# Softmax attention on one core: score products for the maxima on 64 rows with the two heads of a pair side by side, projections moved, the reciprocal packed, the float32 products in one block

## The chip, the cores and the metric

The kernel runs on one core of a Trainium2 chip. The metric is device time in microseconds (us) of one execution; the time of a kernel is the median of its runs. Only one of the kernel's eleven stages, the softmax attention, is changed.

## The reference

A two-layer network on x of 8 batches x 512 tokens x 128 features: a feed-forward layer with 4-bit weights, attention, feed-forward, a mixture of experts, linear attention, a mixture of experts. The changed part is the first attention:

```python
q = split_heads(x @ Wq.T)            # 16 heads of 64
k = split_heads(x @ Wk.T)
v = split_heads(x @ Wv.T)
sim = jnp.einsum('bhid,bhjd->bhij', q, k) * DIM_HEAD ** -0.5
m = jnp.max(sim, axis=-1, keepdims=True)
e = jnp.exp(sim - m)
attn = e / (jnp.sum(e, axis=-1, keepdims=True) + 1e-10)
out = jnp.einsum('bhij,bhjd->bhid', attn, v)
return out.transpose(0, 2, 1, 3).reshape(B, N, INNER) @ Wo.T + bo
```

## The kernel before

`attn_stage` works on 64 pairs of heads (8 batches, 8 pairs each). A pair has 512 queries and 512 keys for each of its two heads. Each engine runs a list of instructions in order, written out by hand as a loop over `PERIODS`; semaphores tie the lists together. In period g the stage works on five pairs at once: it projects pair g+2 (`project`, `high`, `low`, `values_in`, `to_rows`), finds the row maxima of pair g+1 (`scores`, `neg_max`, `max_turned`, `max_row`), computes the exponentials of pair g (`scores_turned`, `exp`), and sums, multiplies with the values and projects out for pairs g-1 and g-2 (`values`, `total_out`, `inv_total`, `normalise`, `output`).

What each of these does:

- `project(g, which)`: q, k or v of the pair as float16 products in high and low parts (three products of 512 columns for q and k, twelve of 128 for v) into the one PSUM bank `proj`. ScalarE's `high` writes the float16 high part, VectorE's `low` the rest, SyncE's `to_rows` copies both by ten DMAs (four of q, four of the high part of k, two of its low part) into `both`, `kh` and `kl`, in which the 128 rows hold high and low parts of a head of 64.
- `scores(g, i)`: one product of 128 queries with 512 keys, eight for a pair, into two banks in turn; VectorE's `neg_max` reduces each. `max_turned` transposes the maxima of a head, VectorE's `max_row` rounds them to `mrow`, and a DMA puts them into row 64 of `both`, so that `scores_turned` subtracts the maximum within its product.
- `scores_turned(g, i)`: keys by queries, two products into one of two banks; ScalarE's `exp` reads it into `pT`. GpSimd adds `pT` up over the keys; `values` sums over the partitions (`sums`), and multiplies `pT` with the values into `pv`, both in float32 on column halves.
- `total_out` copies the sums (128x512, each number repeated on 64 partitions), `inv_total` takes the reciprocal of all of it, `normalise` multiplies, `output` projects and accumulates over the eight pairs of a batch, `add_x` adds to x.

SyncE's list in period g is: `max_row(g, 1)`, the four DMAs of q of pair g+2, `max_row(g+1, 0)`, the six DMAs of k of pair g+2. TensorE's `values` and `output` stand in the middle of a period, after the fourth of eight `scores_turned`.

## Time and profile before

| | us |
|---|---|
| median of 3 runs (2273.93 to 2275.41) | 2275.11 |
| the profiled execution | 2278.47 |
| its span, first to last instruction | 2276.7 |
| TensorE busy in the span | 1866.1 (82%) |
| VectorE busy | 1669.5 (73%) |
| GpSimd busy | 1080.2 (47%) |
| ScalarE busy | 1066.1 (47%) |

The attention stage lies between 252 and 1154 us of the span. PE is TensorE's matmul, PEld its weight loads, DVE VectorE, ACT ScalarE, POOL GpSimd, SPq the instructions with which SyncE issues DMAs. L639 is line 639 of the kernel. A matmul's duration in the profile is longer than its share of the engine, since the next starts before it ends: the distance from one start to the next is what counts. "[0.44 <-ACT ...]" behind a line is the idle time of the engine before it and what ended it.

### The profile page before, as it was taken

The page shows a single profiled execution, that of the slowest core. Times are in us where ns is not written, and L with a number is a line of the kernel's source. Part 1 is how long each engine was busy: PE and PEld are TensorE (multiplying, and loading weights), DVE is VectorE, ACT ScalarE, POOL GpSimd, SP SyncE. Part 2 cuts the span into 40 slices and gives each one's busy share as a digit, 9 for nine tenths or more (in the row PEclk, how much of TensorE's full clock was granted, in tenths as well). Part 3 has the DMA queues.
Part 4 walks back from the last instruction along what each step waited for, and adds up shares of the span by engine and source line. Part 5 has one row for each costly group of instructions (what it writes and reads, how often), then busy time and mean ns, then how long its engine had stood idle before and what let it go on. Part 6 is the DMA issues. An engine that isn't in the chain of part 4 may idle for free. (4 is left out here: it accounts for less than half of the span.)

```text
span 2276.7 us, 36764 instructions
## 1 busy us (share of the span) xinstructions
PE 1866.1 (82%) x12205; PEld 1097.1 (48%) x12205; DVE 1669.5 (73%) x3322; ACT 1066.1 (47%) x2294; POOL 1080.2 (47%) x1304
## 2 busy tenths in 40 slices
PE   0555489999999999999935548999948888789999
PEld 0334234444444444444414435666637677656665
DVE  5887677888788877888778875666667777746665
ACT  0112255555555555555511135555537667445555
POOL 0111255555555555555611134555545556345555
PEclk9888599999999999999968977999979999879999
DMA  6000122222222222222100000000000000000000
GB/s 181 0 0 1 28 56 63 61 59 56 60 60 61 57 57 62 60 61 57 43 0 1 0 1 1 1 0 0 0 0 1 1 1 1 1 1 9 9 9 9
DMA packets 77058, 64.53 MB, mean 28 GB/s; under 512 B 12224, under 2 KB 75904, under 8 KB 76928
## 3 DMA queue, kind: packets, MB, share of 16 engines
q1 hardware_dynamic: 71392, 57.41, 9.9%
q10 hardware_dynamic: 5536, 5.52, 0.8%
q8 instruction: 67, 1.10, 0.2%
q14 instruction: 63, 0.52, 0.1%
HBM read 10.32 MB, written 2.10 MB: 5 GB/s over the span
## 5 line engine op out<-in xcount | busy, mean ns | idle before, releaser
L795 ACT ACTIVATE at_pT<-at_turned 128x512 f32<-128x512 f32 x512 | 305.6, 597 | 292.2 <-PE at_turned L862 273.3
L1022 POOL TENSOR_TENSOR m_g<-m_gT,m_g 128x512 f16<-128x512 f32 x260 | 301.4, 1159 | 232.1 <-ACT m_g L1005 232.1
L1036 PE MATMUL m_h<-m_xT,m_w 128*128 (+1 forms) x1572 | 386.8, 383 | 19.9 <-PEq L463 19.9
L694 DVE TENSOR_REDUCE at_nmax<-at_score 128x1 f32<-128x512 f32 x512 | 337.2, 680 | 71.8 <-PE at_score L839 68.7
L673 POOL TENSOR_TENSOR m_w_attn<-at_pT 128x512 f32<-128x512 f32 x128 | 162.4, 1269 | 377.1 <-ACT at_pT L795 377.1
L972 DVE TENSOR_TENSOR m_gT<-m_silu,m_h 128x512 f32<-128x512 f32 x262 | 180.3, 688 | 200.5 <-ACT m_silu L1001 200.4
L1001 ACT ACTIVATE m_silu<-m_h 128x512 f32<-128x512 f32 x262 | 156.6, 598 | 227.1 <-PE m_h L1036 227.1
L716 DVE RECIPROCAL m_w_attn<-m_w_attn 128x512 f32<-128x512 f32 x64 | 214.6, 3353 | 38.6 <-ACT m_w_attn L801 38.6
L900 PE MATMUL at_pv<-at_pT,at_v 128*64 128x512 f32 x1024 | 231.4, 594 | 0.0
L1055 PEld LDWEIGHTS m_y<-m_w,m_g 128*128 128x128 f16 x3072 | 192.9, 98 | 60.5
L1036 PEld LDWEIGHTS m_h<-m_xT,m_w 128*128 128x128 f16 x1572 | 144.3, 99 | 149.6 <-issue 28.3
L839 PE MATMUL at_score<-at_kh,at_both 128*128 128x512 f16 x512 | 197.1, 385 | 23.5 <-DVE at_nmax L694 16.8
L1055 PE MATMUL m_y<-m_w,m_g 128*128 128x128 f16 x3072 | 213.3, 219 | 0.0
L861 PE MATMUL at_turned<-at_both,at_kh 128*128 128x512 f16 x512 | 195.3, 382 | 0.4 <-ACT at_pT L795 0.3
L862 PE MATMUL at_turned<-at_both,at_kl 128*128 128x512 f16 x512 | 195.3, 381 | 0.0
L681 POOL TENSOR_TENSOR m_w_attn<-m_w_attn,at_pT 128x512 f32<-128x512 f32 x128 | 162.6, 1270 | 11.2 <-ACT at_pT L795 1.3
L677 POOL TENSOR_TENSOR m_w_attn<-m_w_attn,at_pT 128x512 f32<-128x512 f32 x128 | 162.6, 1270 | 10.6 <-ACT at_pT L795 0.8
L1005 ACT CAST m_g<-m_gT 128x512 f16<-128x512 f32 x260 | 158.6, 610 | 0.0
L349 POOL TENSOR_TENSOR f_hq<-f_hg,f_hsc 128x704 f32<-128x704 f32 x32 | 44.4, 1386 | 213.8 <-DVEq L325 213.8
L392 PE MATMUL f_gate<-m_wguT,f_xqT 128*128 128x352 f32 x128 | 61.6, 569 | 102.3 <-DVEq L321 101.0
L900 PEld LDWEIGHTS at_pv<-at_pT,at_v 128*64 128x64 f32 x1024 | 73.7, 138 | 147.6 <-issue 147.6
L987 DVE SCALAR_TENSOR_TENSOR m_x<-m_y,m_we,m_x 128x128 f32 x512 | 143.4, 343 | 0.0
(231 smaller groups left out, 3262.6 us busy)
## 6 DMA issues: line engine op xcount, KB each, us to landing
at_both<-at_part_q SPq DMA_DIRECT2D x128, 128.0 KB, 2.4
at_kh<-at_part_k SPq DMA_DIRECT2D x256, 64.0 KB, 2.0
at_both<-at_part_q SPq DMA_DIRECT2D x128, 64.0 KB, 2.0
at_kl<-at_part_k SPq DMA_DIRECT2D x128, 64.0 KB, 2.0
m_x<-in_x SPq DMA_DIRECT2D x8, 256.0 KB, 4.7
at_both<-at_mrow SPq DMA_DIRECT2D x128, 1.0 KB
out_x<-m_x SPq DMA_DIRECT2D x8, 256.0 KB, 2.3
m_wqkv<-in_w_qkv ACTq DMA_DIRECT2D x1, 1152.0 KB, 6.6
```

Source lines behind the costliest of these rows:

```text
L677: nc.gpsimd.tensor_tensor(acc, acc, pT[g % 2][:, head, 2, :], ALU.add).then_inc(chain, 1)
L694: nc.vector.tensor_reduce(nmax[head][:, qt:qt + 1], score[use % 2][:], AX.X, ALU.max, negate=True)\
L716: nc.vector.reciprocal(rinv, total).then_inc(rinv_done, 1)
L795: nc.scalar.activation(pT[g % 2][:, head, kt, :], turned[i % 2][:], ACT.Exp).then_inc(exp_done, 1)
L839: nc.tensor.matmul(score[use % 2][:], both[k][:, 0, head, qt * P:(qt + 1) * P], kh[k][:, head, :], start=True, stop=True).then_inc(s_done, 1)
L861: nc.tensor.matmul(turned[i % 2][:], kh[k][:, head, tile], both[k][:, 0, head, :], start=True, stop=False)
L862: nc.tensor.matmul(turned[i % 2][:], kl[k][:, head, tile], both[k][:, 1, head, :], start=False, stop=True)\
L900: last = nc.tensor.matmul(pv[halves[head], :], vv[g % 4][:, kt, halves[head]], pT[g % 2][:, head, kt, :], start=(kt == 0), stop=(kt == TPB ...
L972: nc.vector.tensor_tensor(gT[u % 4][:], silu[u % 2][:], h2[u % 2][:], ALU.mult).then_inc(g_done, 1)
L1022: nc.gpsimd.tensor_tensor(g16[u % 4][:, 1, :], gT[u % 4][:], g16[u % 4][:, 0, :], ALU.subtract).then_inc(low_done, 1)
L1036: last = nc.tensor.matmul(bank[:], mem["w12_16"][:, w_part, e, first:first + P], mem["xT"][:, x_part, ds(b * SEQ, SEQ)], start=(i == 0), s ...
L1055: last = nc.tensor.matmul(y[e % 2][:, tile], g16[u % 4][:, g_part, tile], mem["w3_16"][:, w_part, e, j, :], start=(j == 0 and t == 0 and i ...
```

## The change

- `scores` takes q and k from the high parts themselves (`part`, now doubled in a ring of two), 64 rows for each head, the two heads in the two row halves of TensorE and in the two banks. It waits no longer for any DMA. Before, it took q's high and low parts by the high part of k.
- Both heads' maxima go through one `max_turned` (into the bank `sums`), one `max_row` on VectorE and two DMAs, at the end of the period; `scores_turned(g, 0)` waits for both.
- q, v and k are projected after the first, fourth and sixth `scores_turned`. The sums, the output projection, the transposed maxima and the values follow each other at the end of TensorE's period.
- The reciprocal is taken of 32x32 numbers: two DMAs pack the sums, one writes the inverses to DRAM, two spread them over 64 partitions each, in the next period. `normalise` comes one period later.
- The exponents are kept 64 times smaller, and `exp` scales them back.

The core of the diff:

```diff
-        M_UNIT = 64.0
+        SHRINK = 64.0
+        SCALES = (DH ** -0.5 / W_ATTN / 4.0, 1.0 / W_ATTN / 16.0)
...
-        part = [s.sb(f"part_{n}", [P, 2, SEQ], F16) for n in "qk"]
...
-        nmax = [s.sb(f"nmax{i}", [P, P]) for i in range(2)]
-        mrow = [s.sb(f"mrow{i}", [TPB, P], F16) for i in range(2)]
-        oT = [s.sb(f"oT{i}", [P, SEQ]) for i in range(2)]
-        ones = s.sb("ones", [P, DH])
+        nmax = mem["we"][:].rearrange("p t e -> p (t e)")[:, P:2 * P]
+        mrow = s.sb("mrow", [UPP, P], F16)
+        oT = s.sb("oT", [P, SEQ])
+        ones = mem["we"][:].rearrange("p t e -> p (t e)")[:, 0:DH]
+        PACK = 32
+        packed, inv = (s.sb(n, [2 * SEQ // PACK, PACK]) for n in ("packed", "inv"))
+        inv_row = [nc.dram_tensor(f"{tag}_inv_row{i}", [2, SEQ], F32, kind="Internal").ap() for i in range(2)]
...
-        s_in = [s.sem(f"s_in{i}") for i in range(RING)]
+             "added", "sums_done", "total_done", "rinv_done", "pv_done", "o_done", "out_done", "biased", "x_added", "m_done",
+             "m_out", "packed_in", "inv_row_in", "rinv_in"))
         t_in = [s.sem(f"t_in{i}") for i in range(RING)]
-        m_in = [s.sem(f"m_in{i}") for i in range(2)]
-        S_DMAS, T_DMAS = 8, 2
+        m_in = s.sem("m_in")
+        T_DMAS = 10
...
-                    src = part[which]
...
-                def max_row(g, head):
-
-                    sp.wait_ge(s_read, turn_use(g, head) + 1)
-                    sp.dma_start(both[g % RING][DH:DH + 1, 1, head, :].rearrange("o (t q) -> o t q", q=P), mrow[head][:])\
-                      .then_inc(m_in[head], 16)
+                def max_row(g):
+
+                    sp.wait_ge(m_out, g + 1)
+                    for head in range(2):
+                        sp.dma_start(both[g % RING][DH:DH + 1, 1, head, :].rearrange("o (t q) -> o t q", q=P),
+                                     mrow[head * TPB:(head + 1) * TPB, :]).then_inc(m_in, 16)
+
+                packs = [slice(h * SEQ // PACK, (h + 1) * SEQ // PACK) for h in range(2)]
+
+                def pack_total(g):
+
+                    sp.wait_ge(total_done, g + 1)
+                    for h in range(2):
+                        sp.dma_start(packed[packs[h], :], total[h * DH:h * DH + 1, :].rearrange("o (a b) -> o a b", b=PACK))\
+                          .then_inc(packed_in, 16)
+
+                def unpack_inverse(g):
+
+                    sp.wait_ge(rinv_done, g + 1)
+                    if g >= 2:
+                        sp.wait_ge(rinv_in, 32 * (g - 1))
+                    sp.dma_start(inv_row[g % 2].rearrange("h (a b) -> (h a) b", b=PACK), inv[:]).then_inc(inv_row_in, 16)
+
+                def spread_inverse(g):
+
+                    sp.wait_ge(inv_row_in, 16 * (g + 1))
+                    if g:
+                        sp.wait_ge(o_done, g)
+                    for h in range(2):
+                        sp.dma_start(rinv[halves[h], :], inv_row[g % 2][h:h + 1, :].to_broadcast([DH, SEQ])).then_inc(rinv_in, 16)
 
                 sp.wait_ge(set_up, RING + 3)
                 for g in PERIODS:
-                    if live(g):
-                        max_row(g, 1)
+                    if live(g - 2):
+                        spread_inverse(g - 2)
                     if live(g + 2):
                         if g + 2 >= RING:
                             sp.wait_ge(t_done, 8 * (g + 3 - RING))
@@ -653,13 +670,16 @@
                         to_rows(g + 2, 0, 0)
                         sp.wait_ge(lo_done, 2 * (g + 2) + 1)
                         to_rows(g + 2, 0, 1)
-                    if live(g + 1):
-                        max_row(g + 1, 0)
-                    if live(g + 2):
                         sp.wait_ge(hi_done, 2 * (g + 2) + 2)
                         to_rows(g + 2, 1, 0)
                         sp.wait_ge(lo_done, 2 * (g + 2) + 2)
                         to_rows(g + 2, 1, 1)
+                    if live(g - 1):
+                        pack_total(g - 1)
+                    if live(g + 1):
+                        max_row(g + 1)
+                    if live(g - 1):
+                        unpack_inverse(g - 1)
...
-                    head, qt = divmod(i, TPB)
-                    use = score_use(g, i)
-                    dve.wait_ge(s_done, use + 1)
-                    nc.vector.tensor_reduce(nmax[head][:, qt:qt + 1], score[use % 2][:], AX.X, ALU.max, negate=True)\
-                      .then_inc(s_read, 1)
-
-                def max_row(g, head):
-
-                    use = turn_use(g, head)
-                    dve.wait_ge(s_done, use + 1)
+                    qt, head = divmod(i, 2)
+                    col = head * TPB + qt
+                    dve.wait_ge(s_done, UPP * g + i + 1)
+                    nc.vector.tensor_reduce(nmax[:, col:col + 1], score[head][:], AX.X, ALU.max, negate=True).then_inc(s_read, 1)
+
+                def max_row(g):
+
+                    dve.wait_ge(m_done, g + 1)
                     if g:
-                        dve.wait_ge(m_in[head], 16 * g)
-                    nc.vector.tensor_scalar(mrow[head][:], score[use % 2][0:TPB, 0:P], 1.0 / M_UNIT, None, ALU.mult)\
-                      .then_inc(s_read, 1)
+                        dve.wait_ge(m_in, 32 * g)
...
 
                     dve.wait_ge(hi_done, 2 * g + 1 + which)
-                    scale = (DH ** -0.5 / W_ATTN, 1.0 / W_ATTN)[which]
-                    pair = part[which]
+                    scale = SCALES[which]
...
                 def inv_total(g):
-                    dve.wait_ge(total_done, g + 1)
-                    nc.vector.reciprocal(rinv, total).then_inc(rinv_done, 1)
+                    dve.wait_ge(packed_in, 32 * (g + 1))
+                    if g:
+                        dve.wait_ge(inv_row_in, 16 * g)
+                    nc.vector.reciprocal(inv[:], packed[:]).then_inc(rinv_done, 1)
 
                 def normalise(g):
 
                     dve.wait_ge(pv_done, g + 1)
-                    dve.wait_ge(rinv_done, g + 1)
-                    if g >= 2:
-                        dve.wait_ge(out_done, g - 1)
-                    nc.vector.tensor_tensor(oT[g % 2][:], pv[:], rinv, ALU.mult).then_inc(o_done, 1)
...
                 for g in PERIODS:
                     if live(g + 1):
                         neg_max(g + 1, 0)
                         neg_max(g + 1, 1)
-                    if live(g):
-                        max_row(g, 1)
-                    if live(g + 1):
-                        neg_max(g + 1, 2)
-                        neg_max(g + 1, 3)
                     if live(g + 2):
                         low(g + 2, 0)
                     if live(g + 1):
-                        max_row(g + 1, 0)
-                    if live(g + 2):
-                        low(g + 2, 1)
-                    if live(g - 1):
-                        inv_total(g - 1)
-                    if live(g + 1):
-                        neg_max(g + 1, 4)
-                        neg_max(g + 1, 5)
-                    if live(g - 1):
-                        normalise(g - 1)
+                        for i in range(2, 6):
+                            neg_max(g + 1, i)
+                    if live(g - 2):
+                        normalise(g - 2)
                     if live(g + 1):
                         neg_max(g + 1, 6)
                         neg_max(g + 1, 7)
+                    if live(g + 2):
+                        low(g + 2, 1)
+                    if live(g + 1):
+                        max_row(g + 1)
+                    if live(g - 1):
...
-                    act.wait_ge(proj_done, 3 * g + 1 + which)
-                    if g:
-                        act.wait_ge(s_in[(g - 1) % RING], 16 * S_DMAS * ((g - 1) // RING + 1))
-                        act.wait_ge(t_in[(g - 1) % RING], 16 * T_DMAS * ((g - 1) // RING + 1))
-                    scale = (DH ** -0.5 / W_ATTN, 1.0 / W_ATTN)[which]
-                    nc.scalar.mul(part[which][:, 0, :], proj[:], scale).then_inc(hi_done, 1)
+                    act.wait_ge(proj_done, 3 * g + 1 + 2 * which)
+                    if g >= 2:
+                        act.wait_ge(s_done, UPP * (g - 1))
+                        act.wait_ge(t_in[(g - 2) % RING], 16 * T_DMAS * ((g - 2) // RING + 1))
+                    scale = SCALES[which]
...
                 def values_in(g):
-                    act.wait_ge(proj_done, 3 * g + 3)
...
-                    nc.scalar.activation(pT[g % 2][:, head, kt, :], turned[i % 2][:], ACT.Exp).then_inc(exp_done, 1)
+                    nc.scalar.activation(pT[g % 2][:, head, kt, :], turned[i % 2][:], ACT.Exp, scale=SHRINK)\
+                      .then_inc(exp_done, 1)
 
                 def total_out(g):
                     act.wait_ge(sums_done, g + 1)
                     if g:
-                        act.wait_ge(rinv_done, g)
+                        act.wait_ge(packed_in, 32 * g)
...
                 for g in PERIODS:
                     if live(g):
                         exp(g, 0)
-                        exp(g, 1)
-                        exp(g, 2)
                     if live(g + 2):
                         high(g + 2, 0)
                     if live(g):
-                        exp(g, 3)
-                    if live(g + 2):
-                        high(g + 2, 1)
-                    if live(g - 1):
-                        total_out(g - 1)
-                    if live(g):
-                        for i in range(4, 7):
+                        for i in range(1, 4):
                             exp(g, i)
                     if live(g + 2):
                         values_in(g + 2)
                     if live(g):
+                        exp(g, 4)
+                        exp(g, 5)
+                    if live(g + 2):
+                        high(g + 2, 1)
+                    if live(g):
+                        exp(g, 6)
                         exp(g, 7)
+                    if live(g - 1):
+                        total_out(g - 1)
...
-                def bank_free(use):
-                    if use >= 2:
-                        pe.wait_ge(s_read, use - 1)
-
-                def scores(g, i):
-                    head, qt = divmod(i, TPB)
-                    use = score_use(g, i)
-                    k = g % RING
-                    if i == 0:
-                        pe.wait_ge(s_in[k], 16 * S_DMAS * (g // RING + 1))
-                    bank_free(use)
-                    nc.tensor.matmul(score[use % 2][:], both[k][:, 0, head, qt * P:(qt + 1) * P], kh[k][:, head, :], start=True,
-                                     stop=True).then_inc(s_done, 1)
-
-                def max_turned(g, head):
-
-                    use = turn_use(g, head)
-                    pe.wait_ge(s_read, score_use(g, head * TPB + TPB - 1) + 1)
-                    bank_free(use)
-                    nc.tensor.transpose(score[use % 2][:, 0:P], nmax[head][:], mem["ident"][:]).then_inc(s_done, 1)
+                def scores(g, qt):
+
+                    if g and qt == 0:
+                        pe.wait_ge(s_read, UPP * g)
+                    elif qt:
+                        pe.wait_ge(s_read, UPP * g + 2 * qt)
+                    if qt == 0:
+                        pe.wait_ge(lo_done, 2 * g + 2)
+                    q, k = part[g % 2]
+                    for head in range(2):
+                        nc.tensor.matmul(score[head][:], q[halves[head], 0, qt * P:(qt + 1) * P], k[halves[head], 0, :],
+                                         start=True, stop=True).then_inc(s_done, 1)
+
+                def max_turned(g):
+
+                    pe.wait_ge(s_read, UPP * (g + 1))
+                    if g:
+                        pe.wait_ge(m_out, g)
+                    if g >= 2:
+                        pe.wait_ge(total_done, g - 1)
+                    nc.tensor.transpose(sums[:, 0:P], nmax, mem["ident"][:]).then_inc(m_done, 1)
...
-                    if kt == 0:
-                        pe.wait_ge(m_in[head], 16 * (g + 1))
+                    if i == 0:
+                        pe.wait_ge(m_in, 32 * (g + 1))
...
                     if which == 0 and g:
-                        pe.wait_ge(v_out, g)
+                        pe.wait_ge(lo_done, 2 * g)
+                    elif which == 2:
+                        pe.wait_ge(lo_done, 2 * g + 1)
                     elif which == 1:
-                        pe.wait_ge(lo_done, 2 * g + 1)
-                    elif which == 2:
-                        pe.wait_ge(lo_done, 2 * g + 2)
+                        pe.wait_ge(v_out, g + 1)
...
-                def values(g):
+                def key_sums(g):
 
                     pe.wait_ge(added, 2 * (g + 1))
+                    pe.wait_ge(m_out, min(g + 2, PAIRS_ALL))
                     if g:
                         pe.wait_ge(total_done, g)
                     for head in range(2):
-                        last = nc.tensor.matmul(sums[halves[head], :], ones[:], psum[g % 2][:, head, :], start=True, stop=True)
+                        last = nc.tensor.matmul(sums[halves[head], :], ones, psum[g % 2][:, head, :], start=True, stop=True)
                     last.then_inc(sums_done, 1)
+
...
                 pe.wait_ge(set_up, RING + 3)
                 for g in PERIODS:
                     for i in range(UPP):
-                        if live(g + 1):
-                            scores(g + 1, i)
+                        if i % 2 == 0 and live(g + 1):
+                            scores(g + 1, i // 2)
                         if live(g):
                             scores_turned(g, i)
-                        if i == 1 and live(g):
-                            max_turned(g, 1)
-                        if i == 2 and live(g + 2):
-                            project(g + 2, 0)
-                        if i == 3:
-                            if live(g - 2):
-                                output(g - 2)
-                            if live(g + 2):
-                                project(g + 2, 1)
-                            if live(g + 1):
-                                max_turned(g + 1, 0)
-                            if live(g - 1):
-                                values(g - 1)
-                        if i == 6 and live(g + 2):
-                            project(g + 2, 2)
+                        if live(g + 2) and i in (0, 3, 5):
+                            project(g + 2, {0: 0, 3: 2, 5: 1}[i])
+                    if live(g - 1):
+                        key_sums(g - 1)
+                    if live(g - 2):
+                        output(g - 2)
+                    if live(g + 1):
+                        max_turned(g + 1)
+                    if live(g - 1):
+                        values(g - 1)
```

## Rows read from the trace of the kernel before

**Rows 1.** The page: busy tenths of the engines and TensorE's granted clock, 40 slices

```profile
PE   0555489999999999999935548999948888789999
DVE  5887677888788877888778875666667777746665
ACT  0112255555555555555511135555537667445555
PEclk9888599999999999999968977999979999879999
```

**Rows 2.** Busy time of each engine in a stretch of the attention (us)

```profile
600.00:700.00 100.00, 97.55 (x537) 42.97 (x532) 81.19 (x104) 51.81 (x88) 54.34 (x44) 1.00 0.24 61
```

**Rows 3.** The line of the reciprocal, whole span: count, duration ns, first and last start

```profile
L716 DVE RECIPROCAL m_w_attn<-m_w_attn x64: 3352/3353/3354, 303.2 to 1148.0; 128x512 f32<-128x512 f32 x64
```

**Rows 4.** The timeline of one period: start us, us, engine, line, operation, tiles, count

```profile
600.27 3.35 DVE L716 RECIPROCAL m_w_attn<-m_w_attn 128x512 f32<-128x512 f32 x1 [0.44 <-ACT m_w_attn L801]
...
603.19 0.38 PE L861 MATMUL at_turned<-at_both,at_kh 128*128 128x512 f16 x1
603.40 0.38 PE L862 MATMUL at_turned<-at_both,at_kl 128*128 128x512 f16 x1
603.82 1.89 ACT L795 ACTIVATE at_pT<-at_turned 128x512 f32<-128x512 f32 x3 [3.58 <-PE at_turned L862]
...
605.27 2.71 DVE L694 TENSOR_REDUCE at_nmax<-at_score 128x1 f32<-128x512 f32 x4
607.53 0.27 PE L847 MATMUL at_score<-m_ident,at_nmax 128*128 128x128 f32 x1
607.90 0.27 DVE L703 TENSOR_SCALAR at_mrow<-at_score 4x128 f16<-4x128 f32 x1
608.20 0.64 SPq L642 DMA_DIRECT2D at_both<-at_mrow  x1
608.70 0.81 PE L879 MATMUL at_proj<-m_xT,m_w_attn 128*128 128x512 f16 x3
609.55 0.60 ACT L780 ACTIVATE at_part_q<-at_proj 128x512 f16<-128x512 f32 x1
610.00 1.05 PE L912 MATMUL at_out<-m_woT,at_oT 128*128 128x128 f32 x8
610.22 1.28 SPq L630 DMA_DIRECT2D at_both<-at_part_q  x2
...
613.73 3.35 DVE L716 RECIPROCAL m_w_attn<-m_w_attn 128x512 f32<-128x512 f32 x1 [0.44 <-ACT m_w_attn L801]
```

**Rows 5.** The same timeline, SyncE's issues alone

```profile
599.38 0.65 SPq L642 DMA_DIRECT2D at_both<-at_mrow  x1
600.08 0.50 SPq L634 DMA_DIRECT2D at_kh<-at_part_k  x1
600.62 0.60 SPq L635 DMA_DIRECT2D at_kh<-at_part_k  x1
601.26 0.60 SPq L634 DMA_DIRECT2D at_kh<-at_part_k  x1
601.90 0.60 SPq L635 DMA_DIRECT2D at_kh<-at_part_k  x1
602.54 1.23 SPq L637 DMA_DIRECT2D at_kl<-at_part_k  x2
```

**Rows 6.** DMA issues of the page: KB each, median us from issue to landing

```profile
at_kl<-at_part_k SPq DMA_DIRECT2D x128, 64.0 KB, 2.0
m_x<-in_x SPq DMA_DIRECT2D x8, 256.0 KB, 4.7
out_x<-m_x SPq DMA_DIRECT2D x8, 256.0 KB, 2.3
```

**Rows 7.** Groups of DVE lines by shape: busy us, mean ns

```profile
L131 DVE RECIPROCAL f_rscale<-f_hsc 128x44 f32<-128x44 f32 x32 | 13.7, 428 | 1.1
L495 DVE RECIPROCAL n_p<-n_p 128x32 f32<-128x32 f32 x2 | 0.7, 352 | 0.1
```

**Rows 8.** The timeline of TensorE where column halves end and full products begin

```profile
613.74 2.75 PE L900 MATMUL at_pv<-at_pT,at_v 128*64 128x512 f32 x12
616.42 0.39 PE L839 MATMUL at_score<-at_kh,at_both 128*128 128x512 f16 x1
```

**Rows 9.** Busy time by stretch (clock: third last number), at the stage's beginning

```profile
281.00:295.00 14.00, 9.73 (x45) 4.09 (x43) 6.52 (x12) 6.57 (x11) 7.60 (x6) 0.85 0.23 58
```

**Rows 10.** TensorE idle for long: the timeline at both ends of the stage

```profile
294.46 0.39 PE L839 MATMUL at_score<-at_kh,at_both 128*128 128x512 f16 x1 [2.71 <-DMA at_kh<-at_part_k]
295.69 0.63 PE L862 MATMUL at_turned<-at_both,at_kl 128*128 128x512 f16 x1
...
1145.31 1.98 PE L893 MATMUL at_sums<-m_w_attn,at_ones 128*64 128x512 f32 x4 [2.60 <-POOL m_w_attn L681]
```

43 lines of the change are left out of this document (22 added, 21 removed).

## The prediction

> **What bounds the kernel now.** I read the page first. TensorE has nines from slice 7 to slice 19, the attention, at a granted clock of 9 (full) there, with VectorE at seven and eight and ScalarE at five [rows 1]. The busy time by stretch says the same sharper: 97.55 of 100 us for TensorE, 81.19 for VectorE, 51.81 for ScalarE, clock 1.00 [rows 2]. So the attention is bound by TensorE's list, and a change of it must be read there. Next the line of the reciprocal, which runs once a pair: first start 303.2, last 1148.0, so (1148.0 - 303.2)/63 = 13.41 us a pair, and 613.73 - 600.27 = 13.46 in the steady part [rows 3, 4]. Everything below is worked out for one such period and multiplied. Last, SyncE's own list [rows 5], because the change adds most there: this view says what no share of the page says, that a SyncE issue costs 0.64 us whatever it carries.
>
> **What the change saves on TensorE and VectorE.** From one full-width product to the next of 512 columns is 603.40 - 603.19 = 0.21 us [rows 4]. Eight score products become four pairs. If the two row halves run at once, this saves 4 x 0.21 = 0.85 us. The column halves of the values do: 12 products in 2.75 us are six pairs, 0.43 apart ((2.75 - 0.59)/5), and each of the 12 is 0.59 long where a float16 product is 0.38, so that it alone would hold TensorE for 0.42 to 0.43 [rows 4, 8]. If they don't, nothing. I take the saving. VectorE loses the reciprocal of 3.35 us and gets one on 32 columns: 0.35 us [rows 4, 7], and one copy of 0.27 in place of two. So VectorE goes from some 81% to about 60% and can no longer bind for long.
>
> Against it stands the changing of the tile shape. After the last pair of column halves (start 615.89, worked out as 613.74 + 5 x 0.43) the full products could start at 616.32 and start at 616.42 [rows 8]: 0.10 us for one change. The Trainium skill (TensorEngine Tiling, Key Properties) says that changing the tiling mode drains TensorE; the trace agrees, at 0.10 us. Four score pairs among full products make eight changes, 0.8 us by this price, which would eat the 0.85 us. The sum below doesn't rest on it, because of what follows.
>
> **Where the period ends instead.** The maxima of pair g+1 now reach `both` at the very end of SyncE's list, behind the six DMAs of k of pair g+2 and two packing DMAs, and `scores_turned(g+1, 0)`, the second thing on TensorE in the next period, waits for them. Nearly all of TensorE's list is queued behind that wait. This makes a loop, which I walk from the first `scores_turned` (time 0):
>
> 1. ScalarE starts its first exponential 603.82 - 603.19 = 0.63 later, and then one operation each 0.65 ((1.89 - 0.60)/2) [rows 4]. Its list is exp 0, high q, exp 1 to 3, values, exp 4, exp 5, high k. High k is the ninth: 0.63 + 8 x 0.65 = 5.8 if ScalarE never waits.
> 2. It waits once. High q starts at 1.3; VectorE's `low` follows 0.6 after it (0.60 and the step to VectorE) and takes 0.6; only then come reductions 2 and 3 (0.65 each [rows 4]), done at 3.9. The third score pair, the change of shape and the fifth `scores_turned` put exp 4 at 4.9 where its queue alone would have it at 4.5. High k starts at 6.2 and ends at 6.8.
> 3. SyncE issues 610.22 - 609.55 = 0.67 after the start of a high part [rows 4]: at 6.9. From there it has no break: four of `kh`, two of `kl`, two packs, two rows of maxima. The start of the tenth is 0.55 + 7 x 0.64 + 0.69 = 5.7 us behind the first (600.62 - 600.08, 601.26 - 600.62 and 600.08 - 599.38 [rows 5]). The other waits in this list are over by then: low k at about 8.4 against 9.4, the sums' copy at 8.9 against 10.6, the maxima at 9.7 against 11.9.
> 4. The landing: copies between SBUF tiles take 2.0 from the start of the issue [rows 6]. The row of maxima, 4 x 256 bytes, has no landing in this view; it can't take less than an issue (0.65) nor, by the 64 KB copies, much more than 2.0. I take 1.7, since it is the smallest. TensorE then needs 0.1.
>
> Sum: 6.9 + 5.7 + 1.7 + 0.1 = 14.4 us a period, against 13.46.
>
> TensorE's own list would have come round at 13.1. It is through with the eight `scores_turned` at 7.1 (the last waits for exp 5), then sums 0.86 (four records in two steps of 0.43), output 0.89 (its eight records 0.11 apart [rows 4]), the transposed maxima 0.1, values 8 x 0.43 = 3.4, the next score pair 0.2, and four changes of shape 0.4: 13.0 to 13.1. So 1.3 us a period go to waiting at the first `scores_turned`, and the 0.85 saved lies inside that wait: worth nothing.
>
> **The rest.** DMAs a period go from 12 to 17, 10.9 of 14.4 us of SyncE: it still has room. The inverse takes pack (2.0), reciprocal (0.4), issue and write to DRAM (2.3 by the stores of x), two issues and the read (2.0 to 4.7 [rows 6]): `normalise` needs it at 5.7 of the next period and gets it at about 4.6 to 7. SyncE stands in `spread_inverse` until the write has landed and has issued q's four DMAs by 5.5, before high k at 6.9: 1.4 us to spare. The Trainium skill (DMA: Bandwidth & Descriptors, Anatomy of one DMA) puts most of a DMA's fixed 2 us down to the receipt of its write, heaviest for HBM; the stores of x, at 2.3, show little more than SBUF copies do. Ends of the stage: the last pair's inverse makes the trip that nothing hides, about 5 us more than the reciprocal's 3.35, of which other changes at both ends give some 3 back: +2 us. ScalarE, GpSimd and the other ten stages do what they did.
>
> **Sum.** 60 steady periods x (14.4 - 13.46) = 56, and 2 at the ends: +58 us. The profiled execution took 2278.5, so 2336.5; the median of the runs lies 3.4 below it, so 2333.
>
> **Rivals.**
>
> (a) *TensorE stays the bound and the period is 13.1.* It needs SyncE's path from high k to the landed maxima at 6.1 us rather than 7.4, that is issues 0.50 apart in place of 0.64. For it: the first issue of `kh` after each wait is a 0.50 one [rows 5]. Against it: every other of them, small or large, is 0.60 to 0.65. Break-even with before is at 0.54. 60 x (13.1 - 13.46) = -22, and +2: 2255. 13%.
>
> (b) *The wait lets TensorE's clock fall.* Where TensorE idled 2.71 us at the stage's beginning, a product soon after takes 0.63 in place of 0.38, and the granted clock of the stretch is 0.85: it alternated between full (2.4 GHz) and half (1.2); at the end it idled 2.60 [rows 9, 10]. My wait is 1.3, in a period that is otherwise busy, so I expect full clock. If the wait came to 2 us or more, from a longer landing or a smaller list, the products after it (five of 512 columns before ScalarE has what it needs) would cost 0.21 more each, some 1.2 us a period with what follows: 60 x 2.1 = 126, 2403. 12%.
>
> (c) *The inverse's trip binds.* If the write to DRAM lands after 4.7, as loads of x do, q's DMAs end at 8 and k's start 1.1 later: 15.5 a period, 60 x 2.0 = 122, 2400. 6%.
>
> (d) *Row halves don't overlap, or changes of shape cost double.* Then VectorE gets the third score pair 0.2 to 0.3 later, and so does all that follows: 14.6 to 14.7, 2350. This is inside my forecast.
>
> **Chances.** The forecast with (d), 2305 to 2362: 69%; (a) 13%; (b) 12%; (c) 6%. The range reaches down to (a) and stops short of (b) and (c): 2255 to 2385. A measurement of this kernel tells about 0.2% (4.5 us) from no change. Faster 14%, all of it (a); same 4%, between (a) and the forecast; slower 82%.
>
> **What would show it.** In the profile after: the first `scores_turned` of each period idle for 1.0 to 1.6 us before it, and that wait ended by the row of maxima; the distance between reciprocals 14.4; SyncE's ten issues from `kh` to the second row without a break; TensorE below 92% busy in a stretch like rows 2. Score products starting in twos would show the row halves at work. I am wrong if TensorE has no such gap, if the issues stand nearer than 0.55, or if the clock in the attention is not 1.00.

## The result and the profile after

The kernel after takes 2317.27 us (median of 4 runs, 2315.57 to 2318.62), the kernel before 2274.52 in the same rounds (2272.21 to 2275.41): 1.0189 times as long, with a 95% interval of 1.0172 to 1.0207. It is slower, by 43 us where 58 were forecast; the interval leaves open whether that is more or less than 2%. The profiled execution has a span of 2313.8 us against 2276.7, so 37.1 more. The added time lies in one stage: the last addition of the attention is done at 1192.8 where it was done at 1154.2, 38.6 later.

The page, in the rows of [rows 1]: from slice 7 to slice 20 TensorE still shows nines, VectorE has fallen from seven and eight to five, and the clock is full.

```profile
PE   1454589999999999999955556999958888789999
...
DVE  5888655555555555555548885666667777756665
...
PEclk9888599999999999999977786999979999979999
```

The tenths of the page hide what the stretch of [rows 2] shows (busy us of TensorE, weight loads, VectorE, ScalarE, GpSimd; granted clock; DMA share; GB/s): TensorE falls from 97.55 to 92.30, VectorE from 81.19 to 53.11. No engine is full any more.

```profile
600.00:700.00 100.00, 92.30 (x503) 36.49 (x501) 53.11 (x92) 47.08 (x84) 54.84 (x44) 1.00 0.28 75
```

The timeline of a period of the kernel after, which answers to [rows 4] and [rows 5] (start, duration, engine, line, operation; in brackets the idle time before it):

```profile
604.16 0.38 PE L876 MATMUL at_turned<-at_both,at_kh 128*128 128x512 f16 x1 [0.69 <-issue]
604.79 0.60 ACT L808 ACTIVATE at_pT<-at_turned 128x512 f32<-128x512 f32 x1 [5.79 <-PE at_turned L877]
...
605.43 0.60 ACT L793 ACTIVATE at_part_q<-at_proj 128x512 f16<-128x512 f32 x1
605.45 0.38 PE L877 MATMUL at_turned<-at_both,at_kl 128*128 128x512 f16 x1
605.76 0.39 PE L852 MATMUL at_score<-at_part_k,at_part_q 64*128 64x512 f16 x2
...
606.08 0.39 PE L876 MATMUL at_turned<-at_both,at_kh 128*128 128x512 f16 x1
...
608.97 1.09 ACT L808 ACTIVATE at_pT<-at_turned 128x512 f32<-128x512 f32 x2 [0.49 <-PE at_turned L877]
...
610.05 0.60 ACT L793 ACTIVATE at_part_k<-at_proj 128x512 f16<-128x512 f32 x1
...
610.67 0.46 SPq L626 DMA_DIRECT2D at_kh<-at_part_k  x1
611.18 0.60 SPq L627 DMA_DIRECT2D at_kh<-at_part_k  x1
...
613.10 1.24 SPq L629 DMA_DIRECT2D at_kl<-at_part_k  x2
...
614.38 2.27 SPq L644 DMA_DIRECT2D at_packed<-m_w_attn  x2
...
616.69 1.34 SPq L635 DMA_DIRECT2D at_both<-at_mrow  x2
...
619.14 0.38 PE L876 MATMUL at_turned<-at_both,at_kh 128*128 128x512 f16 x1 [1.72 <-issue]
```

The forecast's loop can be read down these lines. The first `scores_turned` starts at 604.16, high k 5.89 later, the first issue of `kh` 0.62 after that; ten issues follow without a break, the last of them some 1.75 before the next first `scores_turned`, which comes after 1.72 us of idle TensorE. Of this period's ten issues one took 1.64 us instead of 0.6 (the two of L644 take 2.27 here and 1.22 in the period before), so the period is 14.98; the median of all is 13.94, the mean 14.12.

### The profile page after: what moved, and what is told of

Same layout as the page of the kernel before. It is cut to its first block and busy times, and to the rows that moved or that the text cites. A ratio compares the mean times of both kernels' runs of the same rounds, so it can differ in the third digit from the quotient of the medians.

```text
span 2313.8 us, 36886 instructions
## 1 busy us (share of the span) xinstructions
PE 1867.3 (81%) x12141; PEld 1057.0 (46%) x12141; DVE 1459.2 (63%) x3257; ACT 1037.9 (45%) x2294; POOL 1078.8 (47%) x1304
## 5 line engine op out<-in xcount | busy, mean ns | idle before, releaser
L808 ACT ACTIVATE at_pT<-at_turned 128x512 f32<-128x512 f32 x512 | 284.5, 595 | 441.2 <-PE at_turned L877 441.2
L714 DVE TENSOR_REDUCE m_we<-at_score 128x1 f32<-128x512 f32 x512 | 328.1, 682 | 53.8 <-PE at_score L852 50.4
L735 DVE RECIPROCAL at_inv<-at_packed 32x32 f32<-32x32 f32 x64 | 21.8, 341 | 196.8 <-DMA at_packed<-m_w_attn 196.8
L876 PEld LDWEIGHTS at_turned<-at_both,at_kh 128*128 128x128 f16 x512 | 49.5, 97 | 170.2 <-issue 105.8
L361 ACT ACTIVATE f_silu<-f_gate 128x704 f32<-128x704 f32 x32 | 24.2, 757 | 228.0 <-PE f_up L393 228.0
```

The costliest lines, as they stand in the source:

```text
L714: nc.vector.tensor_reduce(nmax[:, col:col + 1], score[head][:], AX.X, ALU.max, negate=True).then_inc(s_read, 1)
L808: nc.scalar.activation(pT[g % 2][:, head, kt, :], turned[i % 2][:], ACT.Exp, scale=SHRINK)\
L876: nc.tensor.matmul(turned[i % 2][:], kh[k][:, head, tile], both[k][:, 0, head, :], start=True, stop=False)
```

## The experiments

Each number below that is called a period is the distance between the first `scores_turned` of two successive pairs, as a mean over the 60 periods from pair 2 to pair 62. It is 13.51 in the kernel before and 14.12 in the kernel after (0.60 more before rounding).

**r1: the row of maxima leaves SyncE.** The first question was whether the loop is the cause at all.

```diff
 (SyncE)
-                    if live(g + 1):
-                        max_row(g + 1)
...
 (ScalarE, after total_out)
+                    if live(g + 1):
+                        max_dma(g + 1)
```

> The two DMAs of the maxima are issued by ScalarE at the end of its period, where it is idle, in place of SyncE; nothing else changes. Theory 1 (SyncE's issues from high k to the row of maxima set the period): the path is cut, the wait before the first scores_turned goes, and the period falls from 14.12 us (mean of 60) to what TensorE's list takes, 13.15 (from its first scores_turned at 604.16 to 616.99 + 0.32 with the values and the next score pair back to back): 60 x 0.97 = 58 us less, 2259 us. Theory 2 (the inverse's trip sets it: VectorE stands 2.94 us before the packed reciprocal, and with it the next reductions): the DMAs of that trip stay where they are, so 2310 to 2317. Theory 3 (TensorE's changes of shape around the 64-row products are what costs): unchanged too, 2317.

Measured: 2262.94 us (2260.08 to 2265.49), 0.995 times before (0.9933 to 0.9966); period 13.25. The same work with the same 17 DMAs, two of them issued elsewhere, is 54 us faster than the change and 0.5% faster than before; theory 1 had said 2259, theories 2 and 3 at least 2310. TensorE is full again:

```profile
600.00:700.00 100.00, 98.74 (x541) 39.05 (x539) 59.90 (x104) 53.09 (x95) 59.35 (x47) 1.00 0.30 82
```

**r2: the reciprocal as before.** `pack_total`, `unpack_inverse` and `spread_inverse` go; VectorE takes the 128x512 reciprocal again, behind `o_done`.

```diff
-                    dve.wait_ge(packed_in, 32 * (g + 1))
-                    if g:
-                        dve.wait_ge(inv_row_in, 16 * g)
-                    nc.vector.reciprocal(inv[:], packed[:]).then_inc(rinv_done, 1)
+                    dve.wait_ge(total_done, g + 1)
+                    if g:
+                        dve.wait_ge(o_done, g)
+                    nc.vector.reciprocal(rinv, total).then_inc(rinv_done, 1)
```

> Undoes one part of the change: the reciprocal is again taken of the whole 128x512 on VectorE (3.35 us), at the end of its period; the five DMAs of the pack, the write and the spread go. Theory 1: SyncE's path loses two issues (1.27 us), 13.94 - 1.27 = 12.67, below TensorE's 13.15, so the period is 13.15 and the time 2256 to 2259; VectorE's reciprocal ends at about 13.1 of the period, before the second score pair needs the first two reductions. Theory 2: also faster. Theory 3 (shape changes): 2317. If VectorE's 3.35 us come back as a wait, 2290 or more.

Measured: 2255.73 us (2254.99 to 2258.78), 0.9926 times before (0.9909 to 0.9942), as theory 1 had it; period 13.23. VectorE is back at 79.96 of 100 us and TensorE at the same 98.74 as in r1:

```profile
600.00:700.00 100.00, 98.74 (x541) 38.95 (x538) 79.96 (x102) 52.10 (x93) 58.09 (x47) 1.00 0.24 60
```

So the 20 us per 100 that the packed reciprocal frees on VectorE bought nothing: the period is the same to 0.02 us. What it did was to lengthen SyncE's list. r2 beats r1 by 7 us, of which 5.7 lie behind the last pair (the stage ends 18.9 us after the first `scores_turned` of pair 63 in r2, 24.6 in r1): there the inverse's trip has nothing to hide it.

**r3 and r6: one and three more small issues in SyncE's list**, between the packs and the row of maxima. The loop says that each issue costs its own 0.64 a period.

```diff
+                        sp.dma_start(idle[:], mem["bo"][0:TPB, 0:32]).then_inc(idle_in, 16)
                         max_row(g + 1)
```

> One more DMA of 512 bytes in SyncE's list in each period, between the pack and the row of maxima, into a tile that nobody reads. Theory 1: every period grows by one issue, 0.64 us: 64 x 0.64 = 41 us more, 2358. Theories 2 and 3: it carries nothing that anyone waits for and the list has 3 us of room, so 2317.

Measured, one run: 2363.82 us, 6 above what theory 1 gave. The median period goes from 13.94 to 14.57, that is by 0.63, and its mean to 14.91. Of the 0.79 us that the mean grew, 0.67 lie in SyncE's ten issues, now eleven; another 0.16 in a later high k, behind the six places between 300 and 1130 us where the clock fell. A DMA of a few hundred bytes that nobody on TensorE reads costs 47 us.

> Three more small DMAs in SyncE's list ahead of the row of maxima in each period, in place of one. By the issues alone: 64 x 3 x 0.64 = 123 us above the kernel after, 2440, with the clock at 1.00. If TensorE's wait, now some 2.7 us a period, also lets its clock fall to 1.2 GHz (one more issue, with a wait of 1.4 us and at times 2, made it fall in six places and took 5 us more than the issues), its products behind the wait take twice as long and the period grows by about 1.2 us more: 2490 to 2520.

Measured, one run: 2522.27 us, above the 2440 that the issues alone would give and 2 us beyond the range of the case in which the clock falls. Its stretch and its timeline show how:

```profile
600.00:700.00 100.00, 85.19 (x420) 32.63 (x419) 44.33 (x77) 40.03 (x70) 46.75 (x37) 0.90 0.24 62
```

```profile
611.10 0.39 PE L859 MATMUL at_score<-at_part_k,at_part_q 64*128 64x512 f16 x2
614.19 0.58 PE L883 MATMUL at_turned<-at_both,at_kh 128*128 128x512 f16 x1 [2.70 <-issue]
614.57 0.63 PE L884 MATMUL at_turned<-at_both,at_kl 128*128 128x512 f16 x1
615.00 1.48 PE L901 MATMUL at_proj<-m_xT,m_w_attn 128*128 128x512 f16 x3
...
617.59 0.39 PE L883 MATMUL at_turned<-at_both,at_kh 128*128 128x512 f16 x1
```

After 2.70 us of idling, products of 512 columns take 0.63 us and stand 0.43 apart (half clock, 1.2 GHz) until 617, then 0.39 again (2.4 GHz). So a longer wait is paid twice: once as a wait, and once more as slow products that put the next high k later in the same loop. High k starts 7.16 us after the first `scores_turned` in the median, where it was 5.89. These 1.27 us and the 1.9 of three issues make up the 3.2 by which the period grew, to 17.3.

**r4: one DMA for both rows of maxima.**

```diff
-                    for head in range(2):
-                        sp.dma_start(both[g % RING][DH:DH + 1, 1, head, :].rearrange("o (t q) -> o t q", q=P),
-                                     mrow[head * TPB:(head + 1) * TPB, :]).then_inc(m_in, 16)
+                    sp.dma_start(both[g % RING][DH:DH + 1, 1, :, :].rearrange("o h (t q) -> o (h t) q", q=P), mrow[:])...
```

> The maxima of both heads go by one DMA in place of two. Theory 1: one issue (0.69 us) less in the path: 13.94 - 0.69 = 13.25, still above TensorE's 13.15, so 61 x 0.69 = 42 us less, 2275. Theories 2 and 3: 2317.

Measured: 2278.97 us (2273.65 to 2282.08), 1.002 times before (1.001 to 1.003); period 13.53. One issue fewer is worth 38 us, to 0.2% of the time before. The 4 us above the expected 2275 fit the landing: from the issue to the first `scores_turned` it is 1.84 us in the median for the one DMA, 1.74 for the second of two.

**r9 and r10: what else is in the way?** r9 puts the row of maxima ahead of the packs, so that eight issues instead of ten stand between high k and the maxima.

```diff
-                    if live(g - 1):
-                        pack_total(g - 1)
                     if live(g + 1):
                         max_row(g + 1)
                     if live(g - 1):
+                        pack_total(g - 1)
                         unpack_inverse(g - 1)
```

> On the kernel after, one change: in SyncE's list the two DMAs of the maxima go ahead of the two of the pack. The row of maxima is 1.27 us earlier (path 12.67, TensorE's list 13.15). But the packed sums land that much later, and VectorE stands before the packed reciprocal with the next two reductions behind it: they end at about 16.4 from the first scores_turned, 0.9 after the second score pair wants them, and high k moves with them. So the period stays near 14.0 and the time at 2305 to 2317. If only SyncE's path counts, 2259.

Measured, one run: 2307.5 us, period 13.98. Two issues out of the loop were worth only 10 us, as expected, because another wait takes over. On VectorE the packed reciprocal stands ahead of the next pair's reductions and waits for its packs to land, now 1.3 us later than in the kernel after: VectorE idles 4.32 us before it, and the reductions, on which the second score pair waits, start late.

```profile
604.25 0.34 DVE L734 RECIPROCAL at_inv<-at_packed 32x32 f32<-32x32 f32 x1 [4.32 <-DMA at_packed<-m_w_attn]
604.52 1.21 DVE L713 TENSOR_REDUCE m_we<-at_score 128x1 f32<-128x512 f32 x2
```

r10 puts the packed reciprocal behind these reductions too:

```diff
                         neg_max(g + 1, 1)
+                    if live(g - 2):
+                        inv_total(g - 2)
...
-                    if live(g - 1):
-                        inv_total(g - 1)
```

> As the run before, and the packed reciprocal moves in VectorE's list behind the next period's first two reductions. That wait then holds up nobody; the write to DRAM and the spread come about 1.3 us later, so that q's DMAs end near the time of high k. Period 13.15 to 13.5, 2259 to 2280. If the wait on VectorE wasn't what held the run before, no change against it.

Measured, one run: 2302.96 us, period 13.92. This expectation was wrong by 23 us at least. SyncE's list shows what I had not summed: it has no room left.

```profile
592.78 1.12 SPq L660 DMA_DIRECT2D m_w_attn<-at_inv_row  x2
594.00 1.38 SPq L622 DMA_DIRECT2D at_both<-at_part_q  x2
595.42 1.25 SPq L624 DMA_DIRECT2D at_both<-at_part_q  x2
596.72 0.59 SPq L626 DMA_DIRECT2D at_kh<-at_part_k  x1
...
602.03 1.23 SPq L644 DMA_DIRECT2D at_packed<-m_w_attn  x2
604.79 0.31 SPq L652 DMA_DIRECT2D at_inv_row<-at_inv  x1
606.13 1.14 SPq L660 DMA_DIRECT2D m_w_attn<-at_inv_row  x2
```

From 592.78 to 603.26 it issues sixteen DMAs back to back, not once waiting for q, k or the maxima. Then it waits 1.5 us for the packs to land and be inverted, and 1.0 for the inverse to land in DRAM, and the next round begins at 606.13: 13.35 us. In 49 of the 58 whole rounds between 300 and 1130 us the first fifteen of these 17 steps hold no wait over 0.2 us. The medians of the 17 steps add up to 13.3. Their means add up to the period itself, 13.9, since the steps are the whole round: single issues of 1 to 2 us and a longer wait for the reciprocal make the difference.

**r11: r10 with the packs issued by ScalarE**, to see whether SyncE's list is really what bounds r10.

```diff
 (SyncE)
-                        pack_total(g - 1)
...
 (ScalarE)
                         total_out(g - 1)
+                        pack_total(g - 1)
```

> The kernel of run r10, with one thing moved: the two packing DMAs are issued by ScalarE, right after its copy of the sums, instead of by SyncE; SyncE has 15 issues a period in place of 17. In r10 SyncE stands still only for the two landings of the inverse's trip: the medians of its 17 steps from issue to issue add up to 13.1 us, their means to 13.7, and the period was 13.9. Theory 1, that in r10 SyncE's list is itself the bound: it loses 1.3 us, the period goes to what the rest allows, 13.2 to 13.3 as in r1 and r2, and the time to 2258 to 2268. Theory 2, that r10 is bound by the inverse's trip as a whole (sums, pack, reciprocal, write, spread, `normalise`, and the last two reductions behind it on VectorE): the trip starts no more than 1.4 us earlier and the period stays at 13.6 or above, 2285 to 2300.

Measured: 2280.12 us (2272.88 to 2283.96), 1.0021 times before (1.0008 to 1.0034); period 13.47. It lies below the range of the second theory and above that of the first, so neither was right alone. (The expectation has the 17 steps of r10 at 13.1 and 13.7; counted from start to start they are the 13.3 and 13.9 above.) Taking two issues off SyncE gave 0.45 of the 0.69 us by which r10's period exceeds r2's. Where the rest went can be read from the trace: SyncE's round still has no slack. In 46 of 59 rounds its first thirteen steps hold no wait over 0.2 us, and it stands still only for the inverse (2.67 us in the mean, 1.81 in r10) and for its landing in DRAM (1.1, 1.2 in r10). Of the 1.27 us that two issues take, 0.86 went into the longer wait for the inverse. The packs are now issued early, 5.1 us ahead of the reciprocal in place of 1.75 (medians), but the reciprocal stands behind two reductions in VectorE's list and starts the moment they are through:

```profile
608.56 1.29 DVE L703 TENSOR_REDUCE m_we<-at_score 128x1 f32<-128x512 f32 x2 [3.62 <-PE at_score L853]
609.76 0.33 DVE L724 RECIPROCAL at_inv<-at_packed 32x32 f32<-32x32 f32 x1
610.12 0.32 SPq L643 DMA_DIRECT2D at_inv_row<-at_inv  x1
```

So r11 is bound, as far as its trace tells, by SyncE's issues and the inverse's trip in one round. No run moves the reciprocal in front of the two reductions to show it.

**r5: the score products on all 128 rows**, one head after the other, on the base of r2. It undoes the 64-row pairs alone.

```diff
-                        nc.tensor.matmul(score[head][:], q[halves[head], 0, qt * P:(qt + 1) * P], k[halves[head], 0, :],
+                        nc.tensor.matmul(score[head][:], both[k][:, 0, head, qt * P:(qt + 1) * P], kh[k][:, head, :],
```

> On the kernel with the reciprocal as before (2255.7 us, period 13.21, TensorE 98.7% busy): the score products for the maxima are taken on all 128 rows from the DMAs' tiles, one head after the other, as before the change. If the two row halves at once save what a pair saves (0.21 us each, 0.85 a period), this costs 60 x 0.85 = 51 us: 2307. If the changes of shape around each pair take it back (in the trace of after a pair and what it adds take 0.42 us from the end of the product before to the next start, two full products 0.43), it stays within 6 us of 2256.

Measured: 2274.16 us (2270.72 to 2277.69), 0.9992 times before (0.9983 to 1.0001), 18 us above r2: neither of the two numbers expected. Of these, 4.8 are at the start: the first `scores_turned` is at 286.4 instead of 281.6, since the scores now wait for q's and k's DMAs. The period is 13.44, 0.22 longer, which makes the other 13. Two full products between full ones (r5):

```profile
601.77 0.38 PE L846 MATMUL at_turned<-at_both,at_kh 128*128 128x512 f16 x1
601.99 0.38 PE L847 MATMUL at_turned<-at_both,at_kl 128*128 128x512 f16 x1
...
603.28 0.59 PE L822 MATMUL at_score<-at_kh,at_both 128*128 128x512 f16 x2
603.71 0.38 PE L846 MATMUL at_turned<-at_both,at_kh 128*128 128x512 f16 x1
```

take 603.71 - 603.28 = 0.43 us. In the kernel after, the product of 605.45 would let the next start at 605.67; the pair of row halves starts at 605.76, and full products go on at 606.08: 0.41 with both changes of shape. The halves do run at once, and the two changes eat what this gives. Only where the tile shape changes anyway, behind the values, is the pair a gain: 0.32 us to the next full product against 0.44. That is 0.12 of the 0.22. At the other three places the medians from the last product before a pair to the first full one behind it are 0.635 us in r2 and 0.648 in r5, which makes another 0.04; where the last 0.06 lies I could not read off single products.

r5 also tells what the rest of the change was worth. It keeps the moved projections, the one transposition of the maxima and the float32 block, and its 13.44 is only 0.07 us below the 13.51 of the kernel before (0.03 in the medians); the pairs add 0.22 to that.

**r7 and r8: fewer changes of shape**, both on the base of r2. r7 moves the last score pair next to the sums. r8 leaves it, takes the transposed maxima into a score bank and puts `output` and the transposition ahead of the sums, so that the sums stand beside the values, which have their shape (two changes fewer).

```diff
 (r7)
-                        if i % 2 == 0 and live(g + 1):
+                        if i in (0, 2, 4) and live(g + 1):
                             scores(g + 1, i // 2)
...
+                    if live(g + 1):
+                        scores(g + 1, 3)
                     if live(g - 1):
                         key_sums(g - 1)
 (r8)
-                    if live(g - 1):
-                        key_sums(g - 1)
                     if live(g - 2):
                         output(g - 2)
                     if live(g + 1):
                         max_turned(g + 1)
                     if live(g - 1):
+                        key_sums(g - 1)
                         values(g - 1)
```

> On the kernel with the reciprocal as before: the last score pair moves from before the last two scores_turned to just before the sums, next to another change of shape, so that a period has one change less (0.10 us). VectorE's last reductions come 0.9 us later but still end before the transposed maxima need them (609.8 against 610.2). If a change of shape costs what the gap shows: period 13.21 - 0.10, 60 x 0.10 = 6 us less, 2250. If it costs nothing, 2256; if the later reductions are waited for, more.

> On the kernel with the reciprocal as before (2255.7 us, period 13.21): the maxima are transposed into a score bank, and the output projection and the transpose, which are full products, come before the sums, so that the sums and the values, both on column halves, stand side by side. Two changes of shape fewer in a period (nine in place of eleven). At 0.10 us each: 60 x 0.20 = 12 us less, 2244, which is also below the kernel before by 1.3%. If changes of shape cost nothing: 2256. If the sums, now 1.1 us later, make VectorE's reciprocal late for the second score pair: 2256 or more.

Measured: r7 2249.32 us (2246.99 to 2249.9), 0.9877 times before (0.9861 to 0.9892), period 13.12; r8 2237.53 us (2237.2 to 2239.17), 0.9843 times before (0.9829 to 0.9856), period 12.94. r7 hit. r8 gave 18 us over r2 where 12 were expected, and is the fastest of all. The same block on TensorE, in r2 and in r8:

```profile
607.85 0.38 PE L847 MATMUL at_turned<-at_both,at_kl 128*128 128x512 f16 x1
608.16 1.08 PE L879 MATMUL at_sums<-m_w_attn,m_we 128*64 128x512 f32 x4
609.17 1.16 PE L901 MATMUL at_out<-m_woT,at_oT 128*128 128x128 f32 x8
610.16 0.27 PE L832 MATMUL at_sums<-m_ident,m_we 128*128 128x128 f32 x1
610.37 3.65 PE L889 MATMUL at_pv<-at_pT,at_v 128*64 128x512 f32 x16
613.95 0.39 PE L822 MATMUL at_score<-at_part_k,at_part_q 64*128 64x512 f16 x2
```

```profile
600.16 0.38 PE L846 MATMUL at_turned<-at_both,at_kl 128*128 128x512 f16 x1
600.38 1.05 PE L899 MATMUL at_out<-m_woT,at_oT 128*128 128x128 f32 x8
601.27 0.27 PE L831 MATMUL at_score<-m_ident,m_we 128*128 128x128 f32 x1
601.47 1.08 PE L877 MATMUL at_sums<-m_w_attn,m_we 128*64 128x512 f32 x4
602.38 3.60 PE L887 MATMUL at_pv<-at_pT,at_v 128*64 128x512 f32 x16
605.92 0.39 PE L823 MATMUL at_score<-at_part_k,at_part_q 64*128 64x512 f16 x2
```

From the last full product to the score pair it takes 6.10 us in r2 and 5.76 in r8. The step into the block is 0.31 against 0.22 and the sums' step 1.01 against 0.91: these are the two changes, at 0.1 each. The third 0.1 is in the output (0.99 against 0.89 for its eight products): behind the sums they pay once more, behind a full product they don't. What exactly, the rows don't say.

## Why the prediction was right, and where its sizes were off

**The bound moved where the forecast put it.** Before, TensorE's own list; after, the loop through ScalarE's high k, SyncE's ten issues and the landing of the maxima. r1 takes the row of maxima out of SyncE's list, r4 shortens the list by one issue, r3 and r6 lengthen it by one and three, and nothing else is touched. The times of r1, r4, the kernel after, r3 and r6 follow in this order: 2263, 2279, 2317, 2364, 2522.

**Steps 1 and 2, high k at 6.2: mis-sized.** It starts at 5.89. The course was right: high q at 1.27 (forecast 1.3), fifth exponential at 4.81 (4.9). From there I took 0.65 from one ScalarE operation to the next, read from [rows 4]. But there TensorE gives one pair of `scores_turned` and one score product for each exponential, 3 x 0.21: it was TensorE's pace, not ScalarE's. Where both products are there, two exponentials take 1.09, so they stand 1.09 - 0.60 = 0.49 apart. Steps 1 and 2 together are 0.3 of the 0.46 us that the forecast's period (14.4) lies above the measured median (13.94), and this pace is 0.2 of it; the rest of the 0.46 is small change and rounding in steps 3 and 4.

**Step 3: right.** First issue 0.62 after high k (0.67 forecast), the start of the tenth 5.68 behind the first (5.7) in the median.

**Step 4, a landing of 1.7 and 0.1: right**, at 1.74 together. The packs, the nearest thing with a row, land in 1.7 too.

**The mean is not the median.** 5.89 + 0.62 + 5.68 + 1.74 = 13.93, but the mean period is 14.12, because now and then an issue of SyncE takes longer (26 of 1023 between 300 and 1150 us over 0.9 us, 11 of them over 1.5). A list with no slack passes each of these on. In the kernel before, the same count gives 13.51, not the 13.46 of the one period that I read. So the steady part is 60 x 0.60 = +36 us instead of +56. That 14.4 lies only 0.28 above the mean is partly luck: the loop was taken 0.46 too long, and the long issues, which the forecast had at nothing, gave 0.18 back. Both errors of size are here; the ends, forecast at +2, came to 38.6 - 36 = +2.6, the tail alone to +2.5 (25.05 us from pair 63's first `scores_turned` to the end, against 22.56).

**TensorE's own list, 13.1: right within 0.15.** r1 and r2 have 13.25 and 13.23. The 0.85 us that the pairs save and the 0.8 that eight changes cost stood side by side in the forecast; r5 bears out that most of the saving is eaten: 0.22 us a period is left of it. The Trainium skill (TensorEngine Tiling, Key Properties) says that changing the tiling mode drains TensorE. The runs agree: r7, with one change fewer, is 0.11 us a period shorter, and in r8 each of the two steps that lost a change is 0.1 shorter.

**The inverse's trip was not the bound, and had the room forecast.** Answering to [rows 6], KB each and median us to landing:

```profile
m_w_attn<-at_inv_row SPq DMA_DIRECT2D x128, 128.0 KB, 2.9
...
at_packed<-m_w_attn SPq DMA_DIRECT2D x128, 2.0 KB, 1.7
...
at_inv_row<-at_inv SPq DMA_DIRECT2D x64, 4.0 KB, 1.3
```

The write to DRAM lands in 1.3, not the 2.3 that I took from the stores of x, so rival (c) was far off: q's last issue is done at 608.8, and high k lets SyncE go on at 610.7. The section of the Trainium skill that the prediction cites here (DMA: Bandwidth & Descriptors, Anatomy of one DMA) has HBM as the target with the heaviest receipt, for DMAs that GpSimd issues; of these small ones of SyncE's, the write to DRAM is the quickest, 1.3 us against 1.7 from SBUF to SBUF. What I had not seen is that VectorE stands still for the packs. The reciprocal's own line and the waits of the kernel after from 300 to 1000 us (in all, times, longest) show it:

```profile
L735 DVE RECIPROCAL at_inv<-at_packed 32x32 f32<-32x32 f32 x64 | 21.8, 341 | 196.8 <-DMA at_packed<-m_w_attn 196.8
```

```profile
DVE at_inv L735 <- DMA at_packed<-m_w_attn: 154.6, 50, 4.1
```

VectorE is idle there for 3.1 us a period, nearly the 3.35 that the reciprocal took before [rows 3]. In the kernel after this is hidden behind TensorE's own wait; in r9 it is the next thing late. (VectorE's busy share, forecast at about 60%, is 53. The forecast's own terms say so: 81.19% of 13.46 us is 10.9; less 3.35 and 0.27 and with 0.35 it is 7.7, which is 53% of 14.4.)

**Rivals.** (a), issues 0.50 apart, fell: only the first after a wait is such. (b) is a real mechanism that the change itself doesn't reach: with waits of 0.66 to 2.08 us, 0.68 in the median, the clock stays at 1.00 from 297 us to 1181. With one more issue, r3, it is 0.96 to 0.98 in four of the eight stretches of 100 us from 300 to 1100; it fell behind six waits of 2.02 to 2.87 us, but not behind two of 2.19 and 2.29. In r6, with 2.5 us or more in every period, it is 0.88 to 0.91 in all eight stretches. (d) fell for the price of changes; r5 shows the halves at work. The forecast gave (a) 13% and "faster, all of it (a)" 14%, which should have been one number.

**The signs that I named.** The idle time before the first `scores_turned` is 0.69 and 1.72 in the two periods shown, 0.68 in the median and 0.86 in the mean, against 1.0 to 1.6; the distance between reciprocals 13.94 in the median against 14.4; ten issues without a break, yes; score products starting in twos, yes (both records of 617.03 start together); the clock in the attention 1.00, yes; TensorE below 92% in the stretch, no: 92.30, the same error of 0.46 us seen from the other side.

## What to carry to other kernels

Count the issues of a queue between the last thing that it waits for and the transfer that the bounding engine needs: here each costs about 0.64 us a period, one of 512 bytes in r3 as much as the 64 KB ones, and relieving an engine that doesn't bind (VectorE, 81 to 53%) by five more DMAs turned a gain of 0.7% into a loss of 1.9%. Order the list by who waits, or hand the urgent DMAs to another engine's queue. Half-row tiles pay where the tile shape changes anyway; put operations of one shape side by side before reckoning what a shape saves.

## What the runs showed of the hardware that was not expected

- A SyncE issue takes 0.6 us (median), but one in forty takes 0.9 to 2.0, as the first pack at 614.38 did with 1.64. In a list without slack this adds 0.18 us a period to the median's 13.94.
- A write of 4 KB from SBUF to DRAM lands 1.3 us after the start of its issue, sooner than 2 KB from SBUF to SBUF (1.7).
- Two waits of 2.19 and 2.29 us left TensorE's clock full in r3, while it fell behind six others of 2.02 to 2.87 us in the same run. Each of the six put the next high k at 7.2 us or more in place of 5.89.
- Behind the 64-column float32 sums, eight 128-column float32 products take 0.99 us in place of 0.89, beyond the change of shape itself.
